# The third tile's depthwise convolution in the first layer's tail, divided between TensorE, GpSimd and VectorE

## What is computed

```python
t = relu(bn1(y @ e1_w.T + e1_b))             # 192 -> 384 channels
t = relu(bn2(depthwise_conv(t, e2_w) + e2_b))  # 3x3, pad 1, per channel
t = t @ e3_w.T + e3_b                        # 384 -> 96
s = sigmoid(se2(relu(se1(mean over positions of t))))
x = x + y @ out_proj_w.T + t * s
```

## Time and profile before

| | us |
|---|---|
| median of 3 runs | 27117.58 (27114.8 to 27121.14) |
| the profiled execution, its own time | 27120.91 |
| its span | 27119.1 |
| TensorE, VectorE busy | 24625.3, 24462.1 |
| ScalarE, GpSimd busy | 22561.4, 20690.0 |

### The profile page before, as it was taken

One profiled execution on the slowest core, in us unless ns is written; L12 is line 12 of the kernel. 1 busy time (PEld: TensorE's weight loads), 2 busy tenths in 40 slices (PEclk: granted clock), 3 DMA queues, 4 the chain that ended last, 5 costly groups with the idle time before them and its releaser, 6 DMA issues.

```text
span 27119.1 us, 389769 instructions
## 1 busy us (share of the span) xinstructions
PE 24625.3 (91%) x96900; PEld 13618.6 (50%) x96900; DVE 24462.1 (90%) x17385; ACT 22561.4 (83%) x52277; POOL 20690.0 (76%) x12084
## 2 busy tenths in 40 slices
PE   8999998999999999999989999999999899999999
PEld 4455554555445554555445554445554445544455
DVE  8888988899888998889888999888998988998989
ACT  8777987788777887789778898888988888988888
POOL 8677976778677876778667887777887777977778
PEclk9999999999999999999999999999999999999999
DMA  4443543444443444345434454444544444544444
GB/s 153 124 128 127 166 126 126 128 139 155 124 127 128 158 135 126 127 134 160 126 122 139 147 160 136 136 136 138 160 147 136 137 138 138 169 136 136 137 139 147
DMA packets 1414979, 3764.21 MB, mean 139 GB/s; under 512 B 205408, under 2 KB 205536, under 8 KB 1412064
## 3 DMA queue, kind: packets, MB, share of 16 engines
q1 hardware_dynamic: 1412448, 3736.17, 43.5%
HBM read 3659.85 MB, written 47.19 MB: 137 GB/s over the span
## 4 chain that ended last, share of the span: by engine, by line
PE 33%; issue 23%; DVE 22%; ACT 18%; POOL 3%; DVEq 0%; ACTq 0%; DMA 0%; POOLq 0%; SPq 0%
PE ps L800 13%; DVE ps L1419 8%; DVE arena L1424 8%; ACT arena L1201 8%; ACT arena L1135 4%; PE ps L768 4%; DVE arena L564 3%; PE ps L620 2%; POOL arena L1547 2%; PE ps L788 2%; PE ps L679 1%; PE ps L805 1%; PE ps L806 1%; PE ps L644 1%; PE ps L657 1%
## 5 line engine op out<-in xcount | busy, mean ns | idle before, releaser
L1547 POOL TENSOR_TENSOR arena<-arena 128x768 f32<-128x768 f32 x9216 | 16561.6, 1822 | 1540.1 <-DVE arena L1424 1326.7
L800 PE MATMUL ps<-arena,consts 128*128 128x384 f32 x36864 | 13657.3, 494 | 332.2 <-ACT arena L1235 160.2
L1424 DVE TENSOR_TENSOR_SCAN arena<-arena,carry,ps 128x768 f32<-128x768 f32 x6144 | 10910.4, 1805 | 417.7 <-PE ps L768 262.1
L1135 ACT ACTIVATE arena<-arena,An 128x768 f32<-128x768 f32 x9216 | 8446.3, 930 | 525.8 <-POOL arena L1547 516.7
L800 PEld LDWEIGHTS ps<-arena,consts 128*128 128x128 f32 x36864 | 6329.3, 191 | 4047.0 <-issue 430.9
L1424 DVE TENSOR_TENSOR_SCAN arena<-arena,ps 128x768 f32<-128x768 f32 x3072 | 5286.9, 1746 | 395.2 <-PE ps L768 296.2
L1419 DVE TENSOR_TENSOR ps<-ps,arena 128x768 f32<-128x768 f32 x5216 | 4921.1, 943 | 386.0 <-PE ps L788 381.3
L1201 ACT ACTIVATE arena<-arena 128x64 f32<-128x64 f32 (+1 forms) x14976 | 4266.7, 367 | 583.4 <-PE ps L768 557.0
L768 PE MATMUL ps<-consts,arena 128*128 128x128 f32 x24000 | 3388.7, 278 | 976.5 <-DVE arena L1424 743.8
L1201 ACT ACTIVATE arena<-arena,bT 128x64 f32<-128x64 f32 (+1 forms) x14592 | 4169.6, 368 | 95.9 <-PE ps L768 74.2
L768 PEld LDWEIGHTS ps<-consts,arena 128*128 128x128 f32 x24000 | 2753.5, 142 | 2809.6 <-issue 1678.7
(11 more groups left out here) (184 smaller groups left out, 19541.2 us busy)
## 6 DMA issues: line engine op xcount, KB each, us to landing
arena<-c_rows SPq DMA_DIRECT2D x6144, 384.0 KB, 3.8
arena<-c_rows SPq DMA_DIRECT2D x6144, 192.0 KB, 3.5
arena<-arena SPq DMA_DIRECT2D x384, 72.0 KB, 2.6
c_rows<-arena SPq DMA_DIRECT2D x96, 192.0 KB, 3.1
arena<-x SPq DMA_DIRECT2D x17, 864.0 KB, 4.5
arena<-mid SPq DMA_DIRECT2D x17, 864.0 KB, 4.5
mid<-arena SPq DMA_DIRECT2D x16, 864.0 KB, 3.9
out<-arena SPq DMA_DIRECT2D x16, 864.0 KB, 4.0
```

The lines of the kernel that those rows point to most:

```text
L800: mm = pe.matmul(y_part[:, h, :], ident, hC[it % NH][:, h * SEG:(h + 1) * SEG], start=(n == 0), stop=(n == NS - 1))
L1135: act.activation(state_at[it % NW], delta[g % 2], ACT.Exp, scale=An[:, slot(s) * NS + n:slot(s) * NS + n + 1]).then_inc(sem["da_ready"], 1)
L1424: dve.tensor_tensor_scan(a[:, ::back], a[:, ::back], slots[it % 2][:, ::back], 0.0 if k == 0 else carry[:, n:n + 1], ALU.mult, ALU.add).th ...
L1547: pool.tensor_tensor(hC[it % NH], state_at[it % NW], Csb[b], ALU.mult).then_inc(sem["hc_ready"], 1)
```

## The change

Tile 1's 48 rows are divided 24, 16 and 8 in place of 32 on TensorE and 16 on VectorE. TensorE makes three strips. GpSimd, once its nine diagonals are built and tile 1 of `t1` is complete, makes rows 24 to 39 with nine multiplications and eight additions of 128x768, with two alternating buffers `tapped` for the products; the weight is an operand of width one that is repeated over the rows. VectorE makes rows 40 to 47. ScalarE's relu of the fourth strip, which read PSUM, becomes a relu of GpSimd's rows, in SBUF, and its place is now between the two copies of the projection. Unit `U_CV + 1` is no longer used, and the waits of `claim` are adapted.

```diff
+        tapped = [view(SC + 2 * TT * DM + 9 * P + k * CH, CH) for k in range(2)]
...
+        E2_PE, E2_POOL = 3 * SEGROWS, 5 * SEGROWS
...
-                        return ("t1_ready", k - U_E1 + 1) if k < U_CV else ("t2_ready", k - U_CV + 2)
+                        return ("t1_ready", k - U_E1 + 1) if k < U_CV else ("t1_ready", 6) if k > U_CV else ("t2_ready", 2)
...
-                for g in range(4):
-                    k = U_CV + g // 3
-                    if g % 3 == 0:
-                        claim(k)
+                claim(U_CV)
+                for g in range(3):
                     for tap in range(9):
                         r, dx = g * SEGROWS + tap // 3, tap % 3
-                        mm = pe.matmul(segs(k)[:, g % 3, :], diag[:, tap, :], t1[1][:, r:r + SEGROWS, dx:dx + W],
+                        mm = pe.matmul(segs(U_CV)[:, g, :], diag[:, tap, :], t1[1][:, r:r + SEGROWS, dx:dx + W],
                                        start=(tap == 0), stop=(tap == 8))
-                    if g in (2, 3):
-                        mm.then_inc(sem["unit_full"], 1)
+                mm.then_inc(sem["unit_full"], U_YG - U_CV)
...
-                full(U_CV + 1)
-                second_relu(1, t2[1][:, 3 * SEG:4 * SEG], segs(U_CV + 1)[:, 0, :], 6)
                 keep_unit(U_YG, branch_T, "yg_kept", 0)
+                act.wait_ge(sem["e2_plus"], v("e2_plus", 9))
+                second_relu(1, t2[1][:, E2_PE * W:E2_POOL * W], t2[1][:, E2_PE * W:E2_POOL * W], 6)
                 keep_unit(U_YG, branch_T, "yg_kept", 1)
...
-                second_relu(1, t2[1][:, 4 * SEG:], t2[1][:, 4 * SEG:], 7)
+                second_relu(1, t2[1][:, E2_POOL * W:], t2[1][:, E2_POOL * W:], 7)
...
-                    start = SPLIT1 if t == 1 else 0
+                    start = E2_POOL if t == 1 else 0
...
+                    pool.wait_ge(sem["t1_ready"], v("t1_ready", 4))
+                    planes()
+
+            def planes():
+
+                o = t2[1].rearrange("p (r c) -> p r c", c=W)[:, E2_PE:E2_POOL, :]
+                for tap in range(9):
+                    dy, dx = tap // 3, tap % 3
+                    w = wcol("e2")[:, 9 + tap:10 + tap].unsqueeze(2).to_broadcast([P, E2_POOL - E2_PE, W])
+                    to = tapped[tap % 2].rearrange("p (r c) -> p r c", c=W) if tap else o
+                    if tap >= 3:
+                        pool.wait_ge(sem["e2_plus"], v("e2_plus", tap - 1))
+                    pool.tensor_tensor(to, t1[1][:, E2_PE + dy:E2_POOL + dy, dx:dx + W], w, ALU.mult).then_inc(sem["e2_times"], 1)
+                    if tap:
+                        plus(o, tap - 1)
+                plus(o, 8)
+
+            def plus(o, tap):
+
+                if tap:
+                    pool.wait_ge(sem["e2_times"], v("e2_times", tap + 1))
+                    pool.wait_ge(sem["e2_plus"], v("e2_plus", tap))
+                    pool.tensor_tensor(o, o, tapped[tap % 2].rearrange("p (r c) -> p r c", c=W), ALU.add).then_inc(sem["e2_plus"], 1)
+                else:
+                    pool.wait_ge(sem["e2_times"], v("e2_times", 1))
+                    pool.sem_inc(sem["e2_plus"], 1)
```

More of the change, by code:

```diff
@@ L160 @@
     "z_ready": len(Z_UNITS), "z_copied": len(Z_UNITS), "sz_ready": 2, "merge_ready": NC, "merge_taken": NC, "gated": (0, 4),
-    "t1_cleared": (1, 0), "t1_ready": (6, 0), "e2_diag": (1, 0), "e2_tap": (27, 0), "t2_ready": (5, 0),
+    "t1_cleared": (1, 0), "t1_ready": (6, 0), "e2_diag": (1, 0), "e2_tap": (27, 0), "e2_times": (9, 0), "e2_plus": (9, 0), "t2_ready": (5, 0),
     "se_full": (3, 0), "se_mean": (1, 0), "se_hidden": (1, 0), "se_ready": (1, 0),
```

## The result

The changed kernel takes 27445.4 us (median of 4 runs, 27443.5 to 27446.0), the kernel before 27119.2 (4 runs, 27114.8 to 27121.1): a ratio of 1.012, 95% interval 1.0103 to 1.0138, 326 us slower. The forecast was 27593, range 27230 to 27760. All times and ratios compared here are of fast runs; the one slow run among them, of the kernel with GpSimd on 8 rows (28291 us, its three others 27277 to 27281), is left out.

A forecast was written before the change was run, and what follows sets the result against it. VectorE's taps were taken to bound the tail. Its saving of 3.4 us, 30.3 us of turns with GpSimd and TensorE's later sums made 29.7 us an image, +475 us in 16 on 27120.9: forecast 27593, range 27230 to 27760.

The forecast's parts named there:

- VectorE's part: Convolutions in the tail: tile 1 at 384 instead of 768 elements a tap saves VectorE 3.4 us an image.
- TensorE's part: Tail: dropping the fourth strip frees 5.85 us, 1.5 given back waiting for ScalarE's relu; gain costed at nothing.
- GpSimd's part: Tile 1 in the tail: 17 added instructions, one every 1.78 us, take 30.3 us an image, at most 40.1.
- What the engines cost each other: Taps in the tail: VectorE and GpSimd take turns by whole instructions, adding 30.3 us to VectorE; chance 0.66.
- What is late behind it: Behind the convolutions: relu, copy, e3 and sums make the squeeze-and-excitation step 29.7 us later, VectorE's own end 26.9.
- first rival: Taps in the tail: only about half of each GpSimd instruction delays VectorE, +189 us, 27306 us; chance 0.12.
- No meeting: Taps in the tail: the engines don't contend, VectorE ends 3.4 us earlier an image, 27063 us; chance 0.16.
- third rival: GpSimd in the tail: no contention, but slow operand and windows, 2.36 us an instruction; -27 us, 27091; chance 0.06.

The follow-up runs named there:

- e3: Not a follow-up run: TensorE's work in the tail, in parts and halves, behind the projection's copies and tile 2's relu; 18 records took 8.58 us in the changed kernel.

## Why the prediction was right, and its size off

- **VectorE's part**, 3.4 us: measured 3.40 (50.70 against 54.10).
- **TensorE's part**, worth nothing: right. Its three strips end 1.49 us before the relu that frees the region, as reckoned (1.5), and the freed time became a wait for ScalarE.
- **GpSimd's part**, 1.78 us an instruction: right for the addition (1.82 by its duration), too high for the multiplication with the repeated weight (1.47). The windows of 48 in 50 cost nothing that shows.
- **What the engines cost each other**: the mechanism was right, whole instructions in turn: the tap durations show it, and so do the runs without sums, with fills and with the operand in PSUM. The term was mis-sized: I gave each turn GpSimd's full 1.78 us, and it is 1.10 beside a multiplication and 1.44 beside an addition. Both are 0.37 to 0.38 less than the instruction's own duration; presumably that much of it overlaps with the tap, which no run shows directly. 17 turns make 21.4 us, not 30.3, and line 509 came 72.11 us after the first multiplication, not 81. This term is 8.9 us an image, 142 us, of the 148 between forecast and result.
- **What is late behind it**: I had 2.8 us an image beyond VectorE's own (29.7 - 26.9), and 2.5 were measured. That they agree is luck. The path was right: relu behind GpSimd, second copy, e3 at the low clock. But I had the 18 records of e3 at 9.8 us (3.85 + 6) where they took 8.58, and I overlooked the e3 half behind the sums. In the first image the squeeze-and-excitation step of ScalarE is 1.6 us later beyond the convolutions (79.45 us after the first multiplication against 59.83, less 18.01), and that half makes it another 1.6 at the tiny product (891.57, when the step was done at 889.92).
- **The rivals**: by its number the result lies 139 us from the first rival (27306) and 148 from my forecast, so the time alone doesn't choose between them. Each turn keeps VectorE waiting for three quarters of GpSimd's instruction (1.10 of 1.47, 1.44 of 1.82), between the rival's half and my whole. What speaks for turns is the form: single taps of two fixed lengths, each lengthened by one instruction of GpSimd, by 0.44 and 0.61 us when that has half the elements. No meeting is out for these taps. Its price was right: 27063 reckoned, 27063.0 measured without the sums, and 27064.7 with them where the second operand lies in PSUM. In the third rival the repeated operand was slow, at 2.36 us; it is faster than two full ones (1.47 against 1.82).

The Trainium skill (SBUF — State Buffer, Who interferes with whom) says that a VectorE instruction with two SBUF inputs contends with a GpSimd instruction that reads SBUF and not with one that only writes. The traces agree in both halves: a tap's 2.62 us become 3.70 to 4.05 beside sums, and stay 2.62 beside fills. It also says that a VectorE instruction in a 2-port mode, which `tensor_scalar` can enter, contends with GpSimd, and that whoever issues first holds the shared ports for the whole instruction. The 2.55 us of line 564 beside a fill, for 1.42 alone, bear that out. Where it has the second instruction blocked until the first is through, a turn here cost 0.37 to 0.38 us less than that instruction's duration, and the measurement decides.

## What to carry to other kernels

An idle GpSimd is not free for the other engines. Here its sums cost VectorE's two-operand instructions nothing only where one of the operands lay in PSUM, as in the scan, and its writes alone cost the taps nothing. Price an offload by what each of its instructions adds to VectorE (here its duration less 0.38 us at 768 elements) before counting what it removes: 16 rows on GpSimd let VectorE make 8 rows fewer, which saved it 3.4 us, and cost it 21.4. And when a path is called slack, follow its queue up to the instruction that is waited for, as the tiny product behind half an e3 part showed.

## What the runs showed of the hardware that was not expected

- A GpSimd product of 128x768 with an operand of width one repeated takes 1.47 us, one with two full operands 1.82.
- VectorE's one-operand multiplication (1.42 us for 2304 elements, against a tap's 2.62) waits for GpSimd's fills too (2.55 us), and holds up its additions (2.94 us for 1.82).
- While it waits for its turn, an instruction counts as busy in the profile: GpSimd's additions show 4.11 us, 1.82 without the meeting, and VectorE's busy time rises by 290 us, though it makes fewer rows than before.
- A scan with the same instructions takes from 761.1 to 762.5 us. In the third image the granted clock of its last two stretches of 50 us was 1.00 and 0.97 at 761.2 us, and 0.93 and 0.93 at 762.3. Whatever a change in the tail is worth, this can take back or add some 1.4 us an image, 22 in 16.
